# High parts of the first twelve exponential blocks on GpSimd, and the constant row's additions in the feature stage

## The chip, the cores and the metric

The kernel runs on one core of a Trainium2 chip. The core's engines work side by side, each through its own queue in order, and wait for one another by semaphores: TensorE (PE in the profile; PEld is its weight load), VectorE (DVE), ScalarE (ACT), GpSimd (POOL) and SyncE (SP), which issues most of the DMAs. The metric is the device time of one execution in microseconds (us), lower being better.

## What is computed

A transformer block with two parts, each behind a layer norm and a residual addition: an attention whose scores are distances between three-dimensional positions, causal, with sixteen heads that share them, and a mixture of eight experts with top 2 beside a shared expert. The change touches the attention alone. Cut to it:

```python
x = x + attn(layernorm(x))               # x: (2, 2048, 256)
x = x + ffn(layernorm(x))                # gate, 8 experts, top 2, 2 shared

def attn(x):
    V = x @ wv.T + bv
    pos = x @ w3d.T + b3d                # (2, 2048, 3)
    dist = pairwise_l2(pos)
    scores = -dist * 0.25                # the same for all heads
    scores = where(causal, -inf, scores)
    out = softmax(scores) @ V
    return out @ wo.T + bo
```

All is float32, and the attention's output projection is folded into the value matrix, as the scores are the same for all heads.

## The kernel before

**Tiling.** A batch has S = 2048 tokens, in TB = 16 tiles of 128, four tiles (GT) to a group, GB = 4 groups. The residual stream of both batches stays in `X` in SBUF. The attention runs for batch 0 and then for batch 1 (`for b in range(NB)` on each engine). Products of float32 precision are made of three matmuls on values that are split into a high part, rounded to the type that TensorE reads (fp32r), and a low part, the difference.

**The feature stage.** TensorE transposes and multiplies for values and positions, VectorE and ScalarE split them into `VO`. VectorE then writes 45 small instructions (`N_POS`, each counting up `s_f`) into `FQ`, `FKh` and `FKl`, from which TensorE makes `QT`, `KTh`, `KTl`. In batch 0 VectorE ends this stage with `shift` (L518), the constant row (bias terms) that has to be added to every tile of X.

**The distance stage.** `sq_blocks` lists 40 blocks of squared distances, key tile kt by query group Q, in two halves: Q = 0 and 1, then Q = 2 and 3. TensorE makes one with two matmuls (L658, L659), VectorE evicts it from PSUM into `E` (L523). GpSimd masks the 16 diagonal blocks with two `affine_select` each (`diagonal`, L267 to L274). ScalarE takes the roots of a half row by row (L349) and then the exponentials of that half block by block, in place (L356, `s_exp`).

**The value stage.** `blocks` lists the same 40 blocks in the order of the groups: Q = 0 has 4, Q = 1 has 8, Q = 2 has 12, Q = 3 has 16. They are 512 queries wide, the last four of a group 512, 384, 256 and 128. For each one a high part goes into the ring `E_hi` (NE = 8 buffers) and a low part into `E_lo`, and TensorE multiplies with `VO` (L674, L676, L678: three matmuls for each 128 queries, so 12 for a full block). Who writes the high part depends on the block:

- blocks 0 to 11 (`N_HI_DVE` = 12, the groups of the first half): VectorE, by `split_hi` (L540 to L544), one block ahead of the low part. It counts `s_eh`.
- blocks 12 to 39: ScalarE, by `high_part` (L336 to L340), three blocks behind its exponentials. It counts `s_eh_act`.

The low part of every block is VectorE's (`split_lo`, L546 to L553). Behind a block's low part VectorE may have a `finish` (L525 to L538): when a group's sums are complete, a tile is divided by its denominator, added to X and has its statistics taken. That is done for group Q - 1 within the first three blocks of group Q (two in the third), and needs the tile's constant row added (`s_xc`). A buffer of the ring is free when TensorE has ended the block eight before (`s_eb`, which starts at 8). TensorE's first value matmul stands behind all 40 distance blocks.

In batch 0 VectorE also takes the statistics of batch 1 between the low parts, from block 18 on.

**GpSimd's order in a batch** (L257 to L283): memsets of `FQ`, `FKh`, `FKl` (in batch 1 once batch 0's value stage is over), diagonals 0 to 7, then the constant row's additions for tiles 0 to 11 (`add_shift`, L262 to L265), diagonals 8 to 15, and the additions for tiles 12 to 15. It issues no DMA in the attention.

Of the kernel before, what the change touches and what calls it, by code (L numbers as in the profile page):

```python
# [7 lines left out]
TB = S // P  # L8
GT = 4
# [7 lines left out]
N_FQ, N_FKH, N_POS = 30, 34, 45  # L17
# [34 lines left out]
def attention_and_experts(nc, x, wv, bv, woT, bo, w3dT, b3d, gateT, gate_bias, wT, sw13T, sw2T, out):  # L52
# [19 lines left out]
    with ExitStack() as ctx:  # L72
# [127 lines left out]
        def block_of(Q, kt):  # L200
# [9 lines left out]
        halves = [range(0, GB // 2), range(GB // 2, GB)]  # L210
        sq_blocks = [(Q, kt) for half in halves for kt in range(GT * half[-1] + GT)
                     for Q in range(max(kt // GT, half[0]), half[-1] + 1)]
        N_HI_DVE = blocks.index((halves[1][0], 0))
        AHEAD = 3
        N_STAT = NBLK - 6 - TB
        NROW = sum(GT * half[-1] + GT for half in halves)
# [24 lines left out]
        @block.gpsimd  # L241
        def _(pool):
            pool.memset(ident[:, :], 0.0).then_inc(s_const, 1)
            pool.memset(one_f[:, :], 1.0).then_inc(s_const, 1)
            pool.memset(eps_col[:, :], EPS).then_inc(s_const, 1)
            pool.memset(mean_of[:, :], 1.0 / D).then_inc(s_const, 1)
            pool.memset(w3_raw[:, :, 3:MW - D], 0.0).then_inc(s_const, 1)
            pool.memset(one_zero[:, :, 0], 1.0).then_inc(s_const, 1)
            pool.memset(one_zero[:, :, 1], 0.0).then_inc(s_const, 1)
            pool.memset(blank[:, :], 0.0).then_inc(s_const, 1)  # L250
            pool.iota(no_row[:, :], pattern=[[P, NSLOT]], base=TOPK * NT * P, channel_multiplier=1,
                      allow_small_or_imprecise_dtypes=True).then_inc(s_const, 1)
            pool.wait_ge(s_const, 9)
            pool.memset(blank[:, FIRST:FIRST + 1], -1.0).then_inc(s_const, 1)
            pool.affine_select(out=ident[:, :], in_=ident[:, :], compare_op=ALU.not_equal, fill=1.0, base=0,
                               pattern=[[-1, P]], channel_multiplier=1).then_inc(s_const, 1)
            for b in range(NB):  # L257
                if b > 0:
                    pool.wait_ge(s_eb, b * NBLK + NE)
                for F in (FQ, FKh, FKl):  # L260
                    pool.memset(F[:, :, :], 0.0).then_inc(s_fz, 1)
                def add_shift(tiles):  # L262
                    for t in tiles:
                        pool.tensor_tensor(tile_of(X, b * TB + t), tile_of(X, b * TB + t), shift[:, :], ALU.add)\
                            .then_inc(s_xc, 1)  # L265

                def diagonal(kt):  # L267
                    blk = E[:, off(kt):off(kt) + P]
                    pool.wait_ge(s_e2, b * NBLK + sq_blocks.index((kt // GT, kt)) + 1 + NQ)
                    pool.affine_select(out=blk, in_=blk, compare_op=ALU.is_ge, fill=1.0e30, base=0,  # L270
                                       pattern=[[1, P]], channel_multiplier=-1).then_inc(s_diag, 1)
                    pool.wait_ge(s_diag, 2 * (b * TB + kt) + 1)
                    pool.affine_select(out=blk, in_=blk, compare_op=ALU.not_equal, fill=0.0, base=0,
                                       pattern=[[1, P]], channel_multiplier=-1).then_inc(s_diag, 1)  # L274

                half = GT * len(halves[0])
                for kt in range(half):
                    diagonal(kt)
                pool.wait_ge(s_shift, 1)
                add_shift(range(TB - GT))  # L280
                for kt in range(half, TB):
                    diagonal(kt)
                add_shift(range(TB - GT, TB))  # L283

        @block.scalar
        def _(act):
# [8 lines left out]
            for b in range(NB):  # L295
                def deviation(g0, n):
                    tiles = slice(g0 * GT, (g0 + n) * GT)
                    act.wait_ge(s_mv, TB * b + (g0 + n) * GT)
                    act.activation(std[:, tiles], mv[:, tiles, 1], ACT.Sqrt, bias=eps_col[:, 0:1]).then_inc(s_std, n)

                def group_hi(g):
                    for c in range(KC):
                        act.wait_ge(s_T, KC * (b * GB + g) + c + 1)
                        act.activation(XT_hi[:, g % 2, c, :], T_ps[g % 2][c][:, :], ACT.Copy).then_inc(s_xth, 1)

                group_hi(0)
                if b == 0:
                    deviation(0, 1)
                    for c in range(KC):
                        act.wait_ge(s_Mps, c + 1)  # L310
                        act.activation(M_hi[:, c, 0:D], M_ps[c][:, 0:D], ACT.Copy).then_inc(s_chi, 1)
                else:
                    deviation(0, GB)
                for g in range(GB):
                    if g + 1 < GB:
                        group_hi(g + 1)
                        if b == 0:
                            deviation(g + 1, 1)
                    act.wait_ge(s_rstd, b * GB + g + 1)
                    for j in range(GT):  # L320
                        t = g * GT + j
                        act.wait_ge(s_vps[j % 2], 2 * (b * GB + g) + j // 2 + 1)
                        act.activation(VO[:, t, 0:D], V_ps[j][:, 0:D], ACT.Copy, scale=rstd[:, t:t + 1])\
                           .then_inc(s_voh, 1)
                if b == 0:
                    act.wait_ge(s_bcol, 16)
                    for c in range(KC):
                        act.activation(bv_all[:, c, :], bv_col[:, c:c + 1].to_broadcast([P, P]), ACT.Copy)\
                           .then_inc(s_bv, 1)
                for k, dst in enumerate((QT, KTh, KTl)):  # L330
                    for g in range(GB):
                        n = GB * k + g
                        act.wait_ge(s_ft, 3 * GB * b + n + 1)
                        act.activation(dst[:, g * 512:(g + 1) * 512], Q_ps[n % 4][:, :], ACT.Copy)\
                           .then_inc(s_fr, 1)
                def high_part(n):  # L336
                    blk, _, w = block_of(*blocks[n])
                    act.wait_ge(s_exp, b * NBLK + n + 1)
                    act.wait_ge(s_eb, b * NBLK + n + 1)
                    act.activation(E_hi[:, n % NE, 0:w], blk, ACT.Copy).then_inc(s_eh_act, 1)  # L340

                rows = n = 0
                for half in halves:
                    for kt in range(GT * half[-1] + GT):
                        row = row_of(half, kt)

                        act.wait_ge(s_e2, b * NBLK + sq_blocks.index((half[-1], kt)) + 1 + NQ)
                        act.wait_ge(s_diag, 2 * (b * TB + kt) + 2)
                        act.activation(row, row, ACT.Sqrt).then_inc(s_dist, 1)  # L349
                    rows += GT * half[-1] + GT  # L350

                    act.wait_ge(s_dist, b * NROW + rows)
                    for Q in half:
                        for kt in range(GT * Q + GT):
                            blk = block_of(Q, kt)[0]
                            act.activation(blk, blk, ACT.Exp, scale=-SCALE).then_inc(s_exp, 1)  # L356
                            if n - AHEAD >= N_HI_DVE:
                                high_part(n - AHEAD)
                            n += 1
                for n in range(NBLK - AHEAD, NBLK):  # L360
                    high_part(n)

        @block.vector
        def _(dve):
# [63 lines left out]
            for b in range(NB):  # L428
# [108 lines left out]
                    dve.wait_ge(s_x1, t + 1 + 2 * GT)  # L537
                    dve.bn_stats(st1[:, t, :], tile_of(X, t))  # L538

                def split_hi(n):  # L540
                    blk, _, w = block_of(*blocks[n])
                    dve.wait_ge(s_exp, b * NBLK + n + 1)
                    dve.wait_ge(s_eb, b * NBLK + n + 1)
                    dve.tensor_copy(E_hi[:, n % NE, 0:w], blk).then_inc(s_eh, 1)  # L544

                def split_lo(n):  # L546
                    blk, _, w = block_of(*blocks[n])
                    if n < N_HI_DVE:
                        dve.wait_ge(s_eh, b * N_HI_DVE + n + 1)
                    else:  # L550
                        dve.wait_ge(s_eh_act, (b + 1) * (NBLK - N_HI_DVE) + n + 1 - NBLK)
                    dve.tensor_tensor(E_lo[:, n % NE, 0:w], blk, E_hi[:, n % NE, 0:w].bitcast(f32),  # L552
                                      ALU.subtract).then_inc(s_el, 1)  # L553

                split_hi(0)
                for n, (Q, kt) in enumerate(blocks):
                    if n + 1 < N_HI_DVE:
                        split_hi(n + 1)
                    split_lo(n)
                    if b + 1 < NB and 0 <= n - N_STAT <= TB:  # L560
                        statistics(b + 1, n - N_STAT)
# [945 lines left out]
```

## Time and profile before

| | us |
|---|---|
| time before, median of 3 runs | 629.19 (628.64 to 632.95) |
| the profiled execution's own time | 628.38 |
| its span, first to last instruction | 626.6 |
| granted TensorE clock, mean | 0.961 |

The page of the profile gives, for that execution, the busy time of each engine, the span in 40 slices, the queues, the chain of work that ended last and the costliest groups of instructions. From the trace come timelines (instructions in order of time, equal neighbours merged, with the count behind an x), stretches (busy time of each engine in a given piece of the span) and groups of instructions. Times are us from the span's start. A line number such as L552 is that of the kernel before. An idle time in brackets is the engine's own ahead of the instruction, with what ended it. The attention of batch 0 takes about the first 122 us, that of batch 1 the next 110; the distance stages lie at 46 to 67 and 154 to 175, the value stages behind them.

### The profile page before, as it was taken

Reading aid. Unit: us, or ns where it says so; the run is one execution under the profiler, and the core shown is the slowest. Engines: PE = TensorE matmul, PEld = TensorE weight load, DVE = VectorE, ACT = ScalarE, POOL = GpSimd, SP = SyncE. Lnnn points to the kernel's source line nnn. Section 1 sums busy time; section 2 is a strip of 40 time slices with the busy share of each in tenths; the row PEclk is TensorE's granted clock in tenths of the full one; section 3 lists DMA queues with packets and bytes.
Section 4 is the critical chain, followed back from the end, with each engine's and each line's share of the span. In section 5 each row is a group of like instructions: output and inputs, shape, how many; then the busy total and the mean of one; then the engine's idle time right before and its main releaser. Section 6 shows DMA issues by size and latency. Waiting matters only on the chain.

```text
span 626.6 us, 11501 instructions
## 1 busy us (share of the span) xinstructions
PE 553.8 (88%) x3468; PEld 480.2 (77%) x3468; DVE 452.1 (72%) x1226; ACT 330.2 (53%) x684; POOL 283.5 (45%) x569
## 2 busy tenths in 40 slices
PE   5869799996989979838999998999999999998885
PEld 4856699986579975527888887888888888887764
DVE  7949999584999737586776654666666666664795
ACT  3548978264997805514445432455555555554321
POOL 4007500120840015006676661477667777665690
PEclk9979899997989997977999999899999999999999
DMA  8999000000000009302222222233333333331994
GB/s 266 329 315 14 1 1 2 1 1 2 0 2 1 2 3 378 124 1 86 87 87 87 95 87 61 69 107 109 103 103 107 108 104 109 105 105 60 321 329 155
DMA packets 57130, 63.03 MB, mean 101 GB/s; under 512 B 14737, under 2 KB 50449, under 8 KB 57073
## 3 DMA queue, kind: packets, MB, share of 16 engines
q1 hardware_dynamic: 49216, 43.75, 24.6%
q0 software_dynamic: 6480, 17.90, 8.1%
q10 hardware_dynamic: 1376, 0.66, 0.4%
q8 instruction: 31, 0.51, 0.4%
q14 instruction: 27, 0.21, 0.1%
HBM read 30.64 MB, written 31.65 MB: 99 GB/s over the span
## 4 chain that ended last, share of the span: by engine, by line
PE 54%; DVE 6%; issue 1%; ACT 1%; POOL 0%; DVEq 0%; POOLq 0%
PE bank L1312 16%; PE bank L1314 15%; PE bank L1313 15%; PE bank L1435 3%; PE bank L1451 2%; PE bank L1320 1%; PE bank L1364 1%; DVE h_lo L1242 1%; DVE XN L1086 1%; DVE X L1225 0%; PE bank L1337 0%; DVE X L1215 0%; DVE mv L1083 0%; DVE hf L1234 0%; DVE XT_lo L1124 0%
## 5 line engine op out<-in xcount | busy, mean ns | idle before, releaser
L968 POOL DMA_INDIRECT token_out<-YS,to_row x71 | 71.7, 1010 | 49.4 <-DVE back L1279 46.0
L932 POOL DMA_INDIRECT slots_in<-X,slot x64 | 66.1, 1033 | 60.6 <-DVE slot L1199 30.6
L674 PE MATMUL a_bank<-VO,E_hi 128*128 128x258 f32 x272 | 79.2, 291 | 8.7 <-DVE E_lo L552 6.1
L678 PE MATMUL a_bank<-VO,E_lo 128*128 128x258 f32 x272 | 78.2, 288 | 0.0
L676 PE MATMUL a_bank<-VO,E_hi 128*128 128x256 f32 x272 | 78.0, 287 | 0.0
L1268 DVE TENSOR_TENSOR hr<-bank,sr 128x256 f32<-128x256 f32 x71 | 30.1, 425 | 60.1 <-ACT sr L1045 60.1
L1312 PE MATMUL bank<-W_hi,XST_hi 128*128 x142 | 62.4, 440 | 0.5 <-DVE XST_lo L1284 0.5
L1045 ACT ACTIVATE sr<-bank 128x256 f32<-128x256 f32 x71 | 27.2, 383 | 63.9 <-PE bank L1314 63.9
L674 PEld LDWEIGHTS a_bank<-VO,E_hi 128*128 128x128 f32 x272 | 52.9, 194 | 10.2 <-DVE E_lo L552 7.5
L1019 ACT ACTIVATE h_hi<-hf 128x512 fp32r<-128x512 f32 x32 | 20.2, 632 | 73.2 <-DVE hf L1234 73.2
L1313 PE MATMUL bank<-W_lo,XST_hi 128*128 x142 | 56.8, 400 | 0.0
L1314 PE MATMUL bank<-W_hi,XST_lo 128*128 x142 | 56.3, 397 | 0.0
L1312 PE MATMUL bank<-XT_hi,sw_hi 128*128 128x512 f32 x128 | 51.6, 403 | 3.3 <-DVE XT_lo L1124 1.7
L523 DVE TENSOR_SCALAR E<-a_bank 128x512 f32<-128x512 f32 (+3 forms) x80 | 41.6, 597 | 16.0 <-PE a_bank L659 16.0
L678 PEld LDWEIGHTS a_bank<-VO,E_lo 128*128 128x128 f32 x272 | 52.9, 194 | 0.0
L676 PEld LDWEIGHTS a_bank<-VO,E_hi 128*128 128x128 f32 x272 | 52.8, 194 | 0.0
L1312 PE MATMUL bank<-sw_hi,h_hi 128*128 128x256 f32 x128 | 37.4, 293 | 17.1 <-DVE h_lo L1242 16.0
L1313 PE MATMUL bank<-XT_lo,sw_hi 128*128 128x512 f32 x128 | 50.6, 395 | 0.0
L552 DVE TENSOR_TENSOR E_lo<-E,E_hi 128x512 fp32r<-128x512 f32 (+1 forms) x80 | 48.2, 631 | 3.1 <-ACT E_hi L340 3.1
L1314 PE MATMUL bank<-XT_hi,sw_lo 128*128 128x512 f32 x128 | 50.4, 394 | 0.0
L1312 PE MATMUL bank<-W_hi,hT_hi 128*128 x142 | 45.9, 323 | 0.0
L1057 ACT ACTIVATE YS<-bank,by_weight 128x256 f32<-128x256 f32 x71 | 33.6, 474 | 20.0 <-PE bank L1314 20.0
(247 smaller groups left out, 1680.9 us busy)
## 6 DMA issues: line engine op xcount, KB each, us to landing
XS<-slots_in SPq DMA_DIRECT2D x71, 131.0 KB, 2.1
slots_in<-blank SPq DMA_DIRECT2D x7, 1179.0 KB, 14.0
YG<-token_out SPq DMA_DIRECT2D x16, 512.0 KB, 8.8
W_raw<-in_wT_dram SPq DMA_DIRECT2D x8, 768.0 KB, 13.9
X<-in_x_dram SPq DMA_DIRECT2D x8, 512.0 KB, 8.3
out_dram<-X SPq DMA_DIRECT2D x32, 128.0 KB, 1.9
token_out<-YS,to_row POOLq DMA_INDIRECT x71, 2.5
slots_in<-blank SPq DMA_DIRECT2D x1, 1048.0 KB, 14.3
```

What stands on the lines that cost most here:

```text
L523: dve.tensor_scalar(blk, Q_ps[n % NQ][:, 0:w], 0.0, None, ALU.max).then_inc(s_e2, 1)
L552: dve.tensor_tensor(E_lo[:, n % NE, 0:w], blk, E_hi[:, n % NE, 0:w].bitcast(f32), ALU.subtract).then_inc(s_el, 1)
L674: pe.matmul(O_ps[Q % 2][j][:, 0:D + 2], E_hi[:, n % NE, cols], VO[:, kt, 0:D + 2], start=(kt == 0), stop=False)
L676: pe.matmul(O_ps[Q % 2][j][:, 0:D], E_hi[:, n % NE, cols], VO[:, kt, D + 2:VW], start=False, stop=False)
L678: mm = pe.matmul(O_ps[Q % 2][j][:, 0:D + 2], E_lo[:, n % NE, cols], VO[:, kt, 0:D + 2], start=False, stop=(kt == qt))
L932: pool.indirect_dma_start(out=xs, out_offset=bass.IndirectOffsetOnAxis(ap=slot[k][:, t:t + 1], axis=0), in_=X[:, t, :], in_offset=None).th ...
L968: pool.indirect_dma_start(out=ys, out_offset=bass.IndirectOffsetOnAxis(ap=to_row[:, i:i + 1], axis=0), in_=YS[:, i % NYS, :], in_offset=No ...
L1057: act.activation(YS[:, i % NYS, :], Y_ps[v][:, 0:D], ACT.Copy, scale=by_weight[:, i:i + 1])\
L1268: dve.tensor_tensor(hr[:, v, :], S_ps[v][:, D:2 * D], sr[:, v, :], ALU.mult).then_inc(s_hr, 1)
L1312: pe.matmul(out, a_hi, b_hi, start=start, stop=False, **kw)
L1313: pe.matmul(out, a_hi, b_lo, start=False, stop=False, **kw)
L1314: return pe.matmul(out, a_lo, b_hi, start=False, stop=stop, **kw)
```

## The change

GpSimd gets a function `high_part` that copies a block of E into `E_hi`, with the waits that `split_hi` had. It writes the high parts of blocks 0 to 11 of each batch, and `split_hi` is gone from VectorE, where only the low parts stay. GpSimd's order in a batch becomes: memsets; then a wait for all 45 feature instructions of the batch and for `shift`; additions for tiles 0 to 11; diagonals 0 to 7; additions for tiles 12 to 15; high parts 0 to 7; diagonals 8 to 15; high parts 8 to 11. The constant is renamed to `N_HI_POOL`, its value 12 stays.

```diff
--- before.py
+++ after.py
@@ -210,7 +210,7 @@
         halves = [range(0, GB // 2), range(GB // 2, GB)]
         sq_blocks = [(Q, kt) for half in halves for kt in range(GT * half[-1] + GT)
                      for Q in range(max(kt // GT, half[0]), half[-1] + 1)]
-        N_HI_DVE = blocks.index((halves[1][0], 0))
+        N_HI_POOL = blocks.index((halves[1][0], 0))
         AHEAD = 3
         N_STAT = NBLK - 6 - TB
         NROW = sum(GT * half[-1] + GT for half in halves)
@@ -273,14 +273,25 @@
                     pool.affine_select(out=blk, in_=blk, compare_op=ALU.not_equal, fill=0.0, base=0,
                                        pattern=[[1, P]], channel_multiplier=-1).then_inc(s_diag, 1)
 
+                def high_part(n):
+                    blk, _, w = block_of(*blocks[n])
+                    pool.wait_ge(s_exp, b * NBLK + n + 1)
+                    pool.wait_ge(s_eb, b * NBLK + n + 1)
+                    pool.tensor_copy(E_hi[:, n % NE, 0:w], blk).then_inc(s_eh, 1)
+
                 half = GT * len(halves[0])
+                pool.wait_ge(s_f, N_POS * (b + 1))
+                pool.wait_ge(s_shift, 1)
+                add_shift(range(TB - GT))
                 for kt in range(half):
                     diagonal(kt)
-                pool.wait_ge(s_shift, 1)
-                add_shift(range(TB - GT))
+                add_shift(range(TB - GT, TB))
+                for n in range(NE):
+                    high_part(n)
                 for kt in range(half, TB):
                     diagonal(kt)
-                add_shift(range(TB - GT, TB))
+                for n in range(NE, N_HI_POOL):
+                    high_part(n)
 
         @block.scalar
         def _(act):
@@ -354,7 +365,7 @@
                         for kt in range(GT * Q + GT):
                             blk = block_of(Q, kt)[0]
                             act.activation(blk, blk, ACT.Exp, scale=-SCALE).then_inc(s_exp, 1)
-                            if n - AHEAD >= N_HI_DVE:
+                            if n - AHEAD >= N_HI_POOL:
                                 high_part(n - AHEAD)
                             n += 1
                 for n in range(NBLK - AHEAD, NBLK):
@@ -537,25 +548,16 @@
                     dve.wait_ge(s_x1, t + 1 + 2 * GT)
                     dve.bn_stats(st1[:, t, :], tile_of(X, t))
 
-                def split_hi(n):
-                    blk, _, w = block_of(*blocks[n])
-                    dve.wait_ge(s_exp, b * NBLK + n + 1)
-                    dve.wait_ge(s_eb, b * NBLK + n + 1)
-                    dve.tensor_copy(E_hi[:, n % NE, 0:w], blk).then_inc(s_eh, 1)
-
                 def split_lo(n):
                     blk, _, w = block_of(*blocks[n])
-                    if n < N_HI_DVE:
-                        dve.wait_ge(s_eh, b * N_HI_DVE + n + 1)
+                    if n < N_HI_POOL:
+                        dve.wait_ge(s_eh, b * N_HI_POOL + n + 1)
                     else:
-                        dve.wait_ge(s_eh_act, (b + 1) * (NBLK - N_HI_DVE) + n + 1 - NBLK)
+                        dve.wait_ge(s_eh_act, (b + 1) * (NBLK - N_HI_POOL) + n + 1 - NBLK)
                     dve.tensor_tensor(E_lo[:, n % NE, 0:w], blk, E_hi[:, n % NE, 0:w].bitcast(f32),
                                       ALU.subtract).then_inc(s_el, 1)
 
-                split_hi(0)
                 for n, (Q, kt) in enumerate(blocks):
-                    if n + 1 < N_HI_DVE:
-                        split_hi(n + 1)
                     split_lo(n)
                     if b + 1 < NB and 0 <= n - N_STAT <= TB:
                         statistics(b + 1, n - N_STAT)
```

## Rows read from the trace of the kernel before

**Rows 1.** The page, part 1: busy us (share of span), instructions by engine.

```profile
PE 553.8 (88%) x3468; PEld 480.2 (77%) x3468; DVE 452.1 (72%) x1226; ACT 330.2 (53%) x684; POOL 283.5 (45%) x569
```

**Rows 2.** Stretch of batch 0, behind block 7's start: busy by engine, clock.

```profile
84.00:119.00 35.00, 35.00 (x295) 35.00 (x294) 28.99 (x84) 22.44 (x45) 0.00 (x0) 1.00 0.00 1
```

**Rows 3.** PE's timeline, batch 0: start, duration, line, operation, tiles, count, [idle].

```profile
66.62 0.28 PE L659 MATMUL a_bank<-QT,KTl 128*128 128x128 f32 x1
...
69.49 0.55 PE L674 MATMUL a_bank<-VO,E_hi 128*128 128x258 f32 x1 [2.58 <-issue]
...
70.27 0.42 PE L674 MATMUL a_bank<-VO,E_hi 128*128 128x258 f32 x1
...
71.55 0.42 PE L674 MATMUL a_bank<-VO,E_hi 128*128 128x258 f32 x1
...
81.35 0.39 PE L674 MATMUL a_bank<-VO,E_hi 128*128 128x258 f32 x1 [1.33 <-DVE E_lo L552]
```

**Rows 4.** The same view, batch 1.

```profile
174.87 0.27 PE L659 MATMUL a_bank<-QT,KTl 128*128 128x128 f32 x1
...
177.68 0.39 PE L674 MATMUL a_bank<-VO,E_hi 128*128 128x258 f32 x1 [2.54 <-DVE E_lo L552]
...
189.61 0.39 PE L674 MATMUL a_bank<-VO,E_hi 128*128 128x258 f32 x1 [1.33 <-DVE E_lo L552]
```

**Rows 5.** VectorE's timeline, batch 0, from the evictions to block 18.

```profile
47.19 20.80 DVE L523 TENSOR_SCALAR E<-a_bank 128x512 f32<-128x512 f32 x40 [7.48 <-PE a_bank L659]
67.92 0.77 DVE L544 CAST E_hi<-E 128x512 fp32r<-128x512 f32 x2
68.61 0.77 DVE L552 TENSOR_TENSOR E_lo<-E,E_hi 128x512 fp32r<-128x512 f32 x1
...
72.08 0.82 DVE L552 TENSOR_TENSOR E_lo<-E,E_hi 128x128 fp32r<-128x128 f32 x1
...
78.18 0.16 DVE L532 RECIPROCAL rden<-a_bank 128x1 f32<-128x1 f32 x1
...
79.23 0.15 DVE L532 RECIPROCAL rden<-a_bank 128x1 f32<-128x1 f32 x1
...
89.44 2.48 DVE L552 TENSOR_TENSOR E_lo<-E,E_hi 128x512 fp32r<-128x512 f32 x4
```

**Rows 6.** Short stretches of PE: length, busy, granted clock, DMA, GB/s.

```profile
68.00:69.00 1.00, 0.00 (x0) 0.94 0.03 8
...
72.00:73.00 1.00, 1.00 (x9) 0.85 0.00 0
...
178.00:178.50 0.50, 0.50 (x5) 0.61 0.00 0
```

**Rows 7.** The same view, batch 1: the distance evictions.

```profile
155.43 20.80 DVE L523 TENSOR_SCALAR E<-a_bank 128x512 f32<-128x512 f32 x40 [8.53 <-PE a_bank L659]
```

**Rows 8.** GpSimd's casts of the next stage: count | busy, mean ns | idle.

```profile
L926 POOL CAST sw_hi<-sw_raw 128x2048 fp32r<-128x2048 f32 x1 | 1.9, 1893 | 7.0 <-DMA sw_raw<-in_sw2T_dram 7.0
L926 POOL CAST sw_hi<-sw_raw 128x1024 fp32r<-128x1024 f32 x1 | 1.0, 1039 | 0.0
```

**Rows 9.** Timeline of GpSimd, batch 0.

```profile
48.03 0.29 POOL L270 TENSOR_SCALAR_AFFINE_SELECT E<-E 128x128 f32<-128x128 f32 x1 [40.39 <-DVE E L523]
...
54.45 7.81 POOL L264 TENSOR_TENSOR X<-X,shift 128x256 f32<-128x256 f32 x12
...
63.17 0.29 POOL L270 TENSOR_SCALAR_AFFINE_SELECT E<-E 128x128 f32<-128x128 f32 x1 [0.92 <-DVE E L523]
...
70.36 3.04 POOL L264 TENSOR_TENSOR X<-X,shift 128x256 f32<-128x256 f32 x4
```

**Rows 10.** Timeline of ScalarE, batch 0.

```profile
56.20 5.08 ACT L356 ACTIVATE E<-E 128x512 f32<-128x512 f32 x12
...
62.59 12.28 ACT L349 ACTIVATE E<-E 128x1024 f32<-128x1024 f32 x16
...
78.28 0.62 ACT L340 ACTIVATE E_hi<-E 128x512 fp32r<-128x512 f32 x1
```

## The prediction

> **What bounds the kernel now.** I read the page first: over the whole span PE is busy 88% and VectorE 72% [rows 1], so the change can pay only where PE waits for VectorE. The stretches and timelines of the attention stage say where that is. From block 7 of a batch on, PE is busy without a gap: 35.00 of 35 us with 295 matmuls [rows 2], which gives a pitch of 35.00 / 295 = 0.1186 us at the full clock, or 1.42 us for a block of twelve. Ahead of that it waits. In batch 0 the last distance matmul ends at 66.62 + 0.28 = 66.90, the first value matmul starts only at 69.49, and block 7 starts at 81.35 after a wait of 1.33 for `E_lo` [rows 3]. Blocks 0 to 6 hold 12 + 9 + 6 + 3 + 36 = 66 matmuls, 66 x 0.1186 = 7.83 us of work, yet 81.35 - 69.49 = 11.86 us pass. Batch 1 repeats it: 175.14, 177.68, 189.61 [rows 4].
>
> VectorE is what PE waits for. It evicts the last distance block at about 67.9, then casts two high parts (0.77 for both), writes `E_lo` of block 0 by 69.38, and goes on without idling: cast, `E_lo`, and a `finish` per block [rows 5]. Each 512-wide `E_lo` costs it 0.60 pitch ((2.48 - 0.68) / 3) and each `finish` 79.23 - 78.18 = 1.05 [rows 5]. The seven casts of blocks 1 to 7 and the one of block 0 are the work the change takes off this chain.
>
> One more thing sits there. TensorE's granted clock falls from 2.4 to 1.2 GHz during the wait: at about 68.88 (the 0.94 of the stretch 68 to 69) and back at about 72.30, 3.42 us at half, and in batch 1 from 178.11 [rows 6]. At half clock six matmuls take 71.55 - 70.27 = 1.28, a pitch of 0.213 [rows 3]. Now this is hidden, because VectorE is the slower of the two; afterwards it isn't.
>
> **The change, part by part.**
>
> *1. Twelve casts a batch leave VectorE (L544).* `E_lo` of block 0 becomes the first instruction behind the evictions, at 67.92 [rows 5]. I give it the 0.77 that it takes now with GpSimd's diagonals beside it, and PE starts 0.11 behind its end, as now (69.38 to 69.49): 67.92 + 0.77 + 0.11 = 68.80, so 0.69 earlier. In batch 1 the evictions start at 155.43 and take the same 20.80 [rows 7], so the next instruction is issued 67.92 - 47.19 = 20.73 later, at 176.16, and PE starts at 176.16 + 0.88 = 177.04, or 0.64 earlier.
>
> When could block 7 start? By PE alone at 68.80 + 7.83 = 76.63. By VectorE: `E_lo` of blocks 0 to 4 at 0.60 each (the narrow ones are cheaper, which leaves room for the diagonals), four `finish` (4.20), `E_lo` 5 to 7 (1.80): 67.92 + 3.00 + 4.20 + 1.80 + 0.11 = 77.03. By PE with the clock at half for 3.42 us: 3.42 x (1 - 0.1186 / 0.213) = 1.52 us are lost, 76.63 + 1.52 = 78.15. So batch 0 gains 81.35 - 78.15 = 3.20 if the clock falls in it, 4.32 if it doesn't; batch 1 gains 189.61 - (177.04 + 7.83 + 1.52 = 186.39) = 3.22, or about 4.3.
>
> Will the clock fall? PE's pause shrinks from 2.59 to 1.90 (66.90 to 68.80). In batch 0 it fell 1.98 after the last matmul ended, in batch 1 2.97 after [rows 3, 4, 6]; the pause of 1.33 before block 7 is followed by a clock of 1.00 [rows 2, 3]. The new pause lies between. I take one batch of the two with a fall.
>
> *2. The casts on GpSimd.* The nearest rows are its f32 to fp32r casts of the next stage: 1.89 us for 2048 columns, 1.04 for 1024 [rows 8]. On that line 512 columns cost 0.19 + 512 x 0.00083 = 0.61. Upper bound: its additions of 256 columns, 7.81 / 12 = 0.65 each [rows 9], twice that for 512 with a second operand, 1.30.
>
> Blocks 0 to 7: their exponentials run from 56.20 to 61.28 for twelve, about 59.8 for the eighth [rows 10]. GpSimd is free of its last four additions at 54.45 + 4 x 0.65 = 57.05, and eight casts take at most 8 x 0.61 = 4.9, to 62.0. Diagonal 8 can't start before 63.17 anyway, because its distance block isn't evicted [rows 9]. Cost nothing; the cover is 1.2 us, and behind it another: ScalarE's root of row 8 starts at about 62.59 + 8 x 0.88 = 69.6 (the first rows are the widest, estimated from the merged row's 12.28 for 16) [rows 10]. At 1.30 a cast the diagonals would be 4.3 late and still in time for it.
>
> Blocks 8 to 11 wait for PE to release a buffer, that is for the ends of blocks 0 to 3 (71.3 to 74 with the slow clock), and GpSimd is through its diagonals at 70.36, where its last additions begin now [rows 9]. They end by about 74.6; VectorE wants the first at 77. Hidden. Nothing else is queued behind them until the next batch's memsets, which wait for PE's last block as now.
>
> *3. Contention.* VectorE's `E_lo` of 128 columns took 0.82 at 72.08 [rows 5] with GpSimd's last additions (70.36 to 73.40) beside it [rows 9], against 0.60 for four times the columns when GpSimd is quiet. The casts of blocks 8 to 11 can so hold `E_lo` 5 and 6, at most 0.61 each, and move 77.03 to at most 78.25; the last four additions, which did this until now, are gone from there. A batch whose clock stays up then gains between 3.1 and 4.3, and I take the middle, 3.8 for a warm batch.
>
> The Trainium skill, SBUF — State Buffer, section "SBUF: two separate sides", says that a GpSimd instruction and a VectorE one with two SBUF inputs take a shared port pair in turns, the loser standing still for the whole instruction. The trace agrees (that 0.82). By the rule in full the warm batches gain 3.1 and not 3.8.
>
> *4. The additions of the constant row.* Twelve move ahead of the diagonals. They wait for VectorE's last feature instruction and, in batch 0, for `shift` behind it. VectorE has done both when its idle time ahead of the evictions begins, at 47.19 - 7.48 = 39.71 [rows 5]. The additions take 7.81: to 47.5, with diagonal 0 starting at 48.03 after 40.39 idle [rows 9]. In batch 1 they can start at 155.43 - 8.53 = 146.90 [rows 7] and end at 154.7, before the first eviction. Cost nothing; the cover is 0.5 us in batch 0, and a miss by that much moves only ScalarE, which is 3 us ahead at block 12 (below). No DMA is issued by any moved instruction, and the queues of SP and ACT are not touched.
>
> *5. What comes next.* After block 7 the suppliers must keep 3 to 4 us more ahead. ScalarE's high part of block 12 starts at 78.28 and takes 0.62 [rows 10], its time set by roots and exponentials that don't move; PE wants block 12 at 77.1 + 42 x 0.1186 = 82.1 at the earliest. VectorE from there: `E_lo` 12 at 78.9, then four `finish` and `E_lo` 12 to 15, 4.2 + 2.4 = 6.6, to 85.5; PE wants block 15 at 82.1 + 36 x 0.1186 = 86.4. It holds by 0.9. After that VectorE has 0.60 plus 0.6 of statistics per 1.42. So the gain stays to the end of the batch, and both batches feed one chain.
>
> **Sum.** 3.2 (fallen clock) + 3.8 (clock kept) = 7.0 us off the profiled execution's 628.38 (span 626.6 and 1.8 around it): 621.4. The median shown is 0.81 above that execution, so I forecast 629.19 - 7.0 = 622.2. That is 1.1%; about 1% is what a measurement of this kernel can tell from no change.
>
> **The rivals.**
> *Both clocks fall, or neither.* 3.2 + 3.2 = 6.4 gives 622.8, just over the bound; neither, at the best 4.3 + 4.3 = 8.6, gives 620.6. Same mechanism, other size.
>
> *VectorE is late a second time* (blocks 12 to 15, or `E_lo` 5 to 7 held longer than one cast each). For it: the margin of 0.9. Against: ScalarE's parts are ready 3 us early. If 1 to 2 us a batch are given back: gain 3 to 5, 624.2 to 626.2.
>
> *GpSimd's casts hold the distance evictions.* Eight casts run beside L523, which alone sets the pace of the distance stage. If each held an eviction for its 0.61, a batch would lose 4.9 against 3.2 won: 2 x 1.7 = 3.4 slower, 632.6. It decides from 3.2 / 8 = 0.40 per cast. Against it: twelve additions, which read and write SBUF too, run beside those evictions now, 7.8 us of them, and the clean pitch stays at 0.52 (20.80 for 40) [rows 5, 9].
>
> The Trainium skill, GPSIMD Engine Reference, section "Engine selection", would keep elementwise work on VectorE, with two-input operations about twice as slow on GpSimd and one-input ones near line rate. The trace's 0.00083 us per column for the cast agrees with the second half.
>
> **How the numbers follow.** Forecast with its three clock cases 0.66; given back in part 0.24; slower 0.05; better than all of it 0.05. The low end is 620.6 less 0.6 for the spread of medians, 620.0; the high end reaches the worst of the second rival, 626.2. Faster by over 1% (below 622.9) takes most of the first case, not all, since both-fall lies on the bound: 0.54. Within 1%: 0.42. Slower: 0.04.
>
> **What would show it.** `CAST E_hi` appears on POOL 24 times at about 0.61 for 512 columns and is gone from VectorE; eight of them end before 63.2; L523 still takes 20.8 for 40. First value matmul near 68.8 after a pause of 1.9, block 7 near 77 to 78.2 without a wait ahead of it. It is wrong if the last evictions come later than 67.9, if PE still waits for `E_lo` at blocks 5 to 7, or if a new wait for `E_lo` stands at blocks 12 to 16.

## The result, and the profile after

| | before | after |
|---|---|---|
| median, us | 629.86 (628.64 to 632.95) | 622.37 (621.86 to 623.46) |
| profiled execution, us | 628.38 | 621.86 |
| its span, us | 626.6 | 620.1 |

The ratio is 0.9897 with a 95% interval of 0.9873 to 0.9920, so the changed kernel is 1.0% faster, by 6.5 us. The two medians lie 7.5 apart; the times before scatter by over 4 us, so the ratio is what counts. The median before is now over four executions, one more than in the table of the time before. Six further executions of the changed kernel (e1) gave 0.9901.

The page's first part. VectorE has 24 instructions fewer and GpSimd 24 more; against [rows 1] 11.0 us of busy time left VectorE, more than the casts alone would take undisturbed (0.22 to 0.41 us each, by width, where nothing ran beside them in the trace before; about 8.3 us for all 24):

```profile
PE 552.9 (89%) x3468; PEld 480.1 (77%) x3468; DVE 441.1 (71%) x1202; ACT 329.1 (53%) x684; POOL 291.3 (47%) x593
```

PE's timeline of the changed kernel at the head of the value stage of batch 0, then of batch 1. It answers to [rows 3, 4]. L661 is the distance matmul, L676 the value matmul. The third row of the first view is block 7's first matmul. The pause is 1.80 and 1.75 us where it was 2.58 and 2.54, and behind it there is no wait for `E_lo` any more:

```profile
66.12 0.28 PE L661 MATMUL a_bank<-QT,KTl 128*128 128x128 f32 x1
68.19 0.36 PE L676 MATMUL a_bank<-VO,E_hi 128*128 128x258 f32 x1 [1.80 <-issue]
...
77.68 0.28 PE L676 MATMUL a_bank<-VO,E_hi 128*128 128x258 f32 x1
```

```profile
171.07 0.27 PE L661 MATMUL a_bank<-QT,KTl 128*128 128x128 f32 x1
173.09 0.39 PE L676 MATMUL a_bank<-VO,E_hi 128*128 128x258 f32 x1 [1.75 <-DVE E_lo L557]
```

VectorE's timeline, batch 0, answering to [rows 5]: the same 20.80 us for the 40 evictions, and the low parts of blocks 0 to 4 directly behind them.

```profile
46.69 20.80 DVE L534 TENSOR_SCALAR E<-a_bank 128x512 f32<-128x512 f32 x40 [7.50 <-PE a_bank L661]
67.42 2.66 DVE L557 TENSOR_TENSOR E_lo<-E,E_hi 128x512 fp32r<-128x512 f32 x5
```

GpSimd's timeline, batch 0, answering to [rows 9]. The additions end before diagonal 0, eight casts take 3.87 us, and diagonal 8 still waits, 2.31 us, for its eviction:

```profile
39.34 7.75 POOL L264 TENSOR_TENSOR X<-X,shift 128x256 f32<-128x256 f32 x12 [31.68 <-DVE shift L529]
47.53 0.29 POOL L270 TENSOR_SCALAR_AFFINE_SELECT E<-E 128x128 f32<-128x128 f32 x1 [0.44 <-DVE E L534]
...
56.49 3.87 POOL L280 CAST E_hi<-E 128x512 fp32r<-128x512 f32 x8
62.67 0.29 POOL L270 TENSOR_SCALAR_AFFINE_SELECT E<-E 128x128 f32<-128x128 f32 x1 [2.31 <-DVE E L534]
...
71.05 1.15 POOL L280 CAST E_hi<-E 128x512 fp32r<-128x512 f32 x1 [0.82 <-PE a_bank L680]
```

And the granted clock in short stretches of PE (length, busy and count, clock, DMA share, GB/s), answering to [rows 6]. It falls in both batches, and in both when PE is already back at work: at about 68.42 in batch 0 (0.2 us after the first value matmul) and at about 174.2 in batch 1 (1.1 us after it):

```profile
68.00:69.00 1.00, 0.81 (x5) 0.71 0.00 0
71.00:72.00 1.00, 1.00 (x7) 0.59 0.00 0
173.00:174.00 1.00, 0.91 (x7) 1.00 0.03 8
174.00:175.00 1.00, 1.00 (x8) 0.61 0.00 0
```

**Where the 6.5 us are.** Whole-kernel times scatter by a microsecond or two, and a part of that lies ahead of the first distance stage (its evictions start at 46.69 here, at 47.19 before, and at 47.85 in the same kernel's second profile). A yardstick without that is the length of a value stage, from VectorE's first instruction behind the evictions to PE's first waiting instruction of the next stage. For before that is 124.71 - 67.92 = 56.79 us in batch 0 and 234.77 - 176.16 = 58.61 in batch 1; after, 120.95 - 67.42 = 53.53 and 227.66 - 172.36 = 55.30. The four ends in PE's timelines, before and then after:

```profile
124.71 0.39 PE L598 MATMUL a_bank<-M_hi,XT_hi 128*128 128x260 f32 x1 [1.21 <-DVE XT_lo L397]
...
234.77 1.09 PE L1320 MATMUL bank<-ident,X 128*128 128x128 f32 x8 [3.87 <-POOL before L921]
```

```profile
120.95 0.39 PE L600 MATMUL a_bank<-M_hi,XT_hi 128*128 128x260 f32 x1 [1.21 <-DVE XT_lo L408]
...
227.66 1.09 PE L1322 MATMUL bank<-ident,X 128*128 128x128 f32 x8 [3.87 <-POOL before L923]
```

So the value stages give 3.26 + 3.31 = 6.57 us. Of the rest of the span, the earlier start gives 0.50, and the expert part and the end are about 0.6 longer in this execution, which no edit touches. In the further profiles below, kernels with the same value stage repeat its length within 0.03 us.

### The profile page after: what moved, and what is told of

Read it like the earlier page. It is cut to its first block, busy times and chain, and to the rows that moved or that the text cites. A ratio compares the mean times of both kernels' runs of the same rounds, so it can differ in the third digit from the quotient of the medians.

```text
span 620.1 us, 11503 instructions
## 1 busy us (share of the span) xinstructions
PE 552.9 (89%) x3468; PEld 480.1 (77%) x3468; DVE 441.1 (71%) x1202; ACT 329.1 (53%) x684; POOL 291.3 (47%) x593
## 4 chain that ended last, share of the span: by engine, by line
PE 55%; DVE 6%; issue 1%; ACT 1%; POOL 0%; DVEq 0%; POOLq 0%
PE bank L1314 16%; PE bank L1316 15%; PE bank L1315 15%; PE bank L1437 3%; PE bank L1453 2%; PE bank L1322 1%; PE bank L1366 1%; DVE h_lo L1244 1%; DVE XN L1088 1%; DVE X L1227 0%; PE bank L1339 0%; DVE mv L1085 0%; DVE X L1217 0%; DVE hf L1236 0%; DVE XT_lo L1126 0%
## 5 line engine op out<-in xcount | busy, mean ns | idle before, releaser
L676 PE MATMUL a_bank<-VO,E_hi 128*128 128x258 f32 x272 | 78.5, 289 | 3.5 <-issue 1.8
L676 PEld LDWEIGHTS a_bank<-VO,E_hi 128*128 128x128 f32 x272 | 53.0, 195 | 3.8 <-issue 1.9
L557 DVE TENSOR_TENSOR E_lo<-E,E_hi 128x512 fp32r<-128x512 f32 (+1 forms) x80 | 45.6, 609 | 4.9 <-ACT E_hi L351 4.9
```

The source lines that it names most:

```text
L676: pe.matmul(O_ps[Q % 2][j][:, 0:D + 2], E_hi[:, n % NE, cols], VO[:, kt, 0:D + 2], start=(kt == 0), stop=False)
```

## The experiments

All lengths of the value stages at a glance. "Clock falls" counts the batches in which the granted clock goes to 1.2 GHz at the head of the value stage.

| kernel | batch 0 | batch 1 | clock falls | median, us | ratio to before |
|---|---|---|---|---|---|
| before | 56.79 | 58.61 | 2 | 629.86 | 1 |
| after | 53.53 | 55.30 | 2 | 622.37 | 0.9897 (0.9873 to 0.9920) |
| after again (e1) | 53.55 | 55.33 | 2 | 622.80 | 0.9901 (0.9884 to 0.9918) |
| additions alone (e3) | 54.81 | 56.58 | 2 | 625.18 | 0.9935 (0.9912 to 0.9959) |
| casts alone (e4) | 53.61 | 55.37 | 2 | 623.87 | 0.9910 (0.9891 to 0.9929) |
| casts twice (e6) | 53.57 | 55.37 | 2 | 622.55 | 0.9893 (0.9876 to 0.9909) |
| before, pause filled (e5) | 56.82 | 58.62 | 0 | 630.19 | 1.0015 (1.0004 to 1.0027) |
| additions alone, filled (e8) | 54.81 | 56.57 | 0 | 626.92 | 0.9900 (0.9863 to 0.9938) |
| after, filled with 7 (e2) | 52.09 | 53.89 | 0 | 619.70 | 0.9841 (0.9820 to 0.9863) |
| the same again | 52.10 | 53.89 | 0 | 618.94 | 0.9840 (0.9823 to 0.9857) |
| after, filled with 3 (e9) | 52.11 | 53.87 | 0 | 624.14 | 0.9864 (0.9827 to 0.9900) |
| more pauses filled (e7) | 52.08 | 53.88 | 0 | 616.61 | 0.9792 (0.9773 to 0.9811) |

Each ratio is to the kernel before as it ran beside that run, not to the 629.86 in the table. While e8 and e9 ran the chip was slower and less steady: the kernel before took 632.64 (629.74 to 636.29), and 628.97 and 629.39 beside the others. For these two the ratios and the value stages are to be read, not the medians.

**The changed kernel again (e1).** No edit.

> The changed kernel once more, as the measure for the runs beside it. Theory A (VectorE's casts were PE's limit at the head of each value stage, and what is left there is the half clock): 622 to 623 us, ratio to the kernel before 0.989 to 0.990, PE without a wait for E_lo between block 1 and block 39. In its trace the pause of PE ahead of block 0 is 1.75 to 1.8 us in both batches and the clock falls in or just behind it in most of them.

622.80, ratio 0.9901. The value stages agree with the first profile within 0.03 us, and the clock fell in both batches again.

**The additions alone (e3).** VectorE keeps its casts; GpSimd's order is the new one without the high parts.

```diff
-                for kt in range(half):
-                    diagonal(kt)
+                pool.wait_ge(s_f, N_POS * (b + 1))
                 pool.wait_ge(s_shift, 1)
                 add_shift(range(TB - GT))
-                for kt in range(half, TB):
+                for kt in range(half):
                     diagonal(kt)
                 add_shift(range(TB - GT, TB))
+                for kt in range(half, TB):
+                    diagonal(kt)
```

> The kernel before with only the additions of the constant row moved as in the change; VectorE keeps its casts. Theory A (the casts' time on VectorE is what counts): E_lo and casts at the head of the value stage lose their overlap with GpSimd's last four additions, about 1.4 us of the 0.77 to 0.86 us instructions come back to 0.41 and 0.68; 1.0 to 1.5 us a batch, 2 to 3 us in all, 626.5 to 627.5. Rival D (the gain of the change came from taking GpSimd's additions out of VectorE's way and not from moving the casts): 623 to 624, near the whole gain. Rival E: nothing, 629.

1.98 and 2.03 us less in the value stages, 3.8 in the median: more than theory A's 2 to 3, less than rival D's near-whole gain. VectorE's casts show how. Its timeline in e3 has the casts of blocks 4 and 5, alone on their ports, at 0.41; before, the one that began at 71.30 took 0.86:

```profile
71.92 0.41 DVE L545 CAST E_hi<-E 128x512 fp32r<-128x512 f32 x1
```

```profile
71.30 0.86 DVE L544 CAST E_hi<-E 128x512 fp32r<-128x512 f32 x1
```

PE's waits for low parts in e3 are three, 2.9 us together. 2.5 of these are the pause ahead of block 0 in batch 1; the other two stand ahead of block 7, 0.20 and 0.21 us where there were 1.33. So VectorE still sets the start of block 7, but PE with its fallen clock is almost as late:

```profile
PE a_bank L675 <- DVE E_lo L553: 2.9, 3, 2.5
```

```profile
80.53 0.39 PE L675 MATMUL a_bank<-VO,E_hi 128*128 128x258 f32 x1 [0.20 <-DVE E_lo L553]
```

**The casts alone (e4).** The high parts on GpSimd, the additions where they were.

```diff
-                pool.wait_ge(s_f, N_POS * (b + 1))
-                pool.wait_ge(s_shift, 1)
-                add_shift(range(TB - GT))
                 for kt in range(half):
                     diagonal(kt)
-                add_shift(range(TB - GT, TB))
+                pool.wait_ge(s_shift, 1)
+                add_shift(range(TB - GT))
                 for n in range(NE):
                     high_part(n)
                 for kt in range(half, TB):
                     diagonal(kt)
+                add_shift(range(TB - GT, TB))
```

> The changed kernel with the additions of the constant row where they were before (twelve behind diagonal 7, four behind diagonal 15). GpSimd then runs 7.8 us later: its first high part at about 62.3 and not 57, diagonal 8 at 66.4 and not 63.2, the last additions at 72 to 75, the high part of block 8 at about 75. Theory A (there is cover: ScalarE's root of row 8 comes at 69.6, VectorE's first low part at 67.9, its low part of block 8 at 77): within 1 us of the changed kernel, 622.5 to 623.5, E_lo of blocks 0 to 7 up to 0.3 us longer each while the additions run. Rival D (the move of the additions matters by itself): 1 us a batch or more is lost, above 624.5.

The value stages are 0.08 and 0.07 us longer than with the whole change, which is theory A. The median, 623.87, is 0.4 above theory A's range and 1.1 above e1 beside it; the value stages don't hold that difference, and in the two profiles 1.06 us of it lies ahead of the first eviction (48.91 against 47.85), where no run looked for its cause. The two halves of the change don't add up: additions alone give 2.0 a batch, casts alone 3.2, both together 3.3. Once the casts are gone, VectorE has room to be held up by the additions: in the changed kernel its low part of block 7 starts at 75.67 and takes 0.68, and PE starts on it only at 77.68, 1.3 us later. GpSimd ran as late as expected (its timeline, batch 0: casts at 63.90, the last additions at 74.14, and the four high parts behind them at 77.16), and nobody paid for it: ScalarE waited 2.6 us for its diagonals in batch 0, 3.1 in the changed kernel, and no low part came late for PE:

```profile
56.16 7.79 POOL L264 TENSOR_TENSOR X<-X,shift 128x256 f32<-128x256 f32 x12
63.90 3.87 POOL L280 CAST E_hi<-E 128x512 fp32r<-128x512 f32 x8
...
74.14 3.08 POOL L264 TENSOR_TENSOR X<-X,shift 128x256 f32<-128x256 f32 x4
77.16 2.56 POOL L280 CAST E_hi<-E 128x512 fp32r<-128x512 f32 x4
```

**The casts twice (e6).** The changed kernel with

```diff
+                    pool.tensor_copy(E_hi[:, n % NE, 0:w], blk).then_inc(s_once, 1)
+                    pool.wait_ge(s_once, b * N_HI_POOL + n + 1)
                     pool.tensor_copy(E_hi[:, n % NE, 0:w], blk).then_inc(s_eh, 1)
```

> The changed kernel with each of GpSimd's twelve casts a batch made twice. The first eight then end about 4.4 us later, near 64.8 in the changed kernel's time, and diagonal 8 starts 2 us later than its distance block allows. Theory A (the casts are covered by ScalarE's roots and by the ring): the same as the changed kernel within 0.5 us, 622.3 to 623.3, the 40 evictions still at 20.8. Rival G (a cast on GpSimd holds an eviction or a low part of VectorE): 0.4 to 0.6 us for each of the additional casts beside it, 3 us a batch, 625 or more.

622.55, value stages within 0.07 us of the changed kernel's. Rival G is out: sixteen casts beside the evictions leave them at 20.81 for 40. A 512-wide cast takes 0.61, a 128-wide one 0.29:

```profile
58.87 0.61 POOL L283 CAST E_hi<-E 128x512 fp32r<-128x512 f32 x1
...
61.60 0.29 POOL L283 CAST E_hi<-E 128x128 fp32r<-128x128 f32 x1
```

```profile
48.36 20.81 DVE L537 TENSOR_SCALAR E<-a_bank 128x512 f32<-128x512 f32 x40 [7.57 <-PE a_bank L664]
```

**The pause filled (e2, and again).** Behind the distance loop of TensorE:

```diff
+                for _ in range(7):
+                    pe.matmul(bank[7][:, :], KTh[:, 0:P], QT[:, 0:512], start=True, stop=True)
                 if b == 0:
                     pe.wait_ge(s_shift, 1)
```

> The changed kernel with seven more matmuls of 512 columns behind the last distance block of each batch, into a PSUM bank that nobody reads then; they are work the reference doesn't ask for and fill 7 x 0.23 = 1.6 us of PE's pause of 1.8. Theory A (the half clock is now what the head of the value stage pays, 3.42 us at a pitch of 0.213 and not 0.119, that is 1.5 us a batch): the clock stays at full, block 7 starts 1.1 to 1.5 us earlier in each batch, 2.2 to 3.0 us less in all, 619.3 to 620.2. Rival B (VectorE is at once the limit again, because block 7's E_lo is ready only just before PE wants it): the clock stays at full but PE waits at blocks 5 to 7, and less than 0.8 us is won. Rival C (the clock isn't governed by PE's own pause): it falls all the same, and nothing is won.

> The changed kernel with seven matmuls in the pause ahead of the value stage once more, beside the one that fills more pauses. 619.3 to 620.3; ratio to the kernel before 0.983 to 0.986.

1.44 and 1.41 us less in the value stages than the changed kernel, 3.1 in the median, 0.9841 and 0.9840 of the kernel before (the second median, 618.94, is 0.4 below its range). Rivals B and C are out: the clock is 1.00 at the head of both value stages, and PE is at work for all but 0.1 of ten microseconds. PE's timeline with the filling and the stretches behind it, in the second of the two runs:

```profile
66.56 1.84 PE L664 MATMUL a_bank<-QT,KTh 128*128 128x512 f32 x7
```

```profile
67.00:77.00 10.00, 9.88 (x77) 1.00 0.01 2
169.00:179.00 10.00, 9.93 (x75) 1.00 0.01 2
```

But rival B's condition is nearly met. In the first of the two runs VectorE's low part of block 7, the first of the five in this row, ends at 77.79 + 0.68 = 78.47, and PE starts on the block at 78.54, 0.07 us later (the same in batch 1). So with the clock kept the two engines arrive together, and a PE faster still would win next to nothing here:

```profile
77.79 2.28 DVE L557 TENSOR_TENSOR E_lo<-E,E_hi 128x512 fp32r<-128x512 f32 x5
```

```profile
78.54 0.36 PE L678 MATMUL a_bank<-VO,E_hi 128*128 128x258 f32 x1
```

**The same in the kernel before (e5)**, with ten matmuls for its longer pause.

> The kernel before with ten matmuls of 512 columns behind the last distance block of each batch (work the reference doesn't ask for, into a bank nobody reads then), 10 x 0.23 = 2.3 us of PE's pause of 2.6. Theory A (there VectorE is the slower one at the head of the value stage, so the half clock of TensorE is hidden): the clock stays at full and the time is that of the kernel before within 0.5 us, with longer waits of PE for E_lo between block 1 and block 7. Rival F (the half clock was already paid before the change): 2 to 3 us less.

Value stages +0.03 and +0.01, ratio 1.0015 (median 0.8 above the kernel before beside it, where 0.5 was allowed; the value stages don't show it). The clock stays at full, and PE only waits more. Before and then in e5, its waits for low parts; 2.54 of the 6.1 are the pause ahead of block 0 in batch 1, so 3.5 became 5.5:

```profile
PE a_bank L674 <- DVE E_lo L552: 6.1, 6, 2.5
```

```profile
PE a_bank L676 <- DVE E_lo L552: 5.5, 9, 1.3
```

So the half clock cost nothing before the change and costs 1.4 us a batch after it.

**The additions alone, pause filled (e8)**, the edits of e3 and e5 together.

> The kernel before with the additions moved (VectorE keeps its casts) and ten matmuls more in PE's pause of 2.6 us. It tells what the casts themselves are worth once the clock is kept. Theory A: with the casts on VectorE its chain sets block 7 (its low part at 79.8 + 0.68 in the run with the additions moved alone, PE's own time there with a full clock 1.5 us earlier), so the kept clock brings less than 0.5 us a batch: 624.3 to 625.3, and the casts on GpSimd are then worth 2.5 us a batch, the difference to the changed kernel with its pause filled (618.9 to 619.7). Rival H (PE's pace with the half clock is the limit in that kernel too): 1.5 us a batch less, 622 to 622.5, and the casts are worth 1.3 a batch as without the filling.

The value stages are those of e3 to 0.01 us. With the casts on VectorE its chain is the limit, clock or no clock; rival H is out. PE waits 1.3 us for block 7's low part again:

```profile
PE a_bank L677 <- DVE E_lo L553: 3.0, 4, 1.3
```

Against e2 the casts are worth 54.81 - 52.09 = 2.72 and 2.68 us a batch when the clock is kept, and 1.28 (54.81 - 53.53) when it falls. The ratio, 0.9900, came out better than e3's 0.9935 and by itself would fit rival H; their intervals overlap, the value stages rule H out, and a part of the difference lies between the two value stages (50.87 us against 51.54 in e3), where in the feature stage of batch 1 the clock falls 1.8 us and returns 1.4 us earlier.

**Three matmuls and not seven (e9).** `range(3)`.

> The changed kernel with three matmuls and not seven in the pause, 0.7 us of 1.8, so that PE still rests 1.1 us ahead of the value stage. If a rest of 1.1 us is short enough for the clock (PE's rests of 1.0 to 1.3 us ahead of the distance stage are followed by a full clock) the clock stays at full and the time is that with seven, 619 to 620. If it falls in one batch or both, 620.5 to 622.5.

Value stages as with seven, ratio 0.9864 (0.9827 to 0.9900; the seven had 0.984). After a rest of 1.05 us in batch 0 and 1.00 in batch 1 the clock stays at full:

```profile
69.62 0.36 PE L678 MATMUL a_bank<-VO,E_hi 128*128 128x258 f32 x1 [1.05 <-issue]
```

**More pauses filled (e7).** On top of e2, 8 matmuls of 260 columns ahead of the first transpose of the position maximum, and 18 (batch 0) or 28 (batch 1) behind its spreading:

```diff
+                for _ in range(8):
+                    pe.matmul(bank[7][:, 0:MW], XT_hi[:, 1, 0, 0:P], M_hi[:, 0, :], start=True, stop=True)
                 pe.wait_ge(s_f, N_POS * b + 1)
...
+                for _ in range(28 if b > 0 else 18):
+                    pe.matmul(bank[7][:, 0:MW], XT_hi[:, 1, 0, 0:P], M_hi[:, 0, :], start=True, stop=True)
                 for k, (F, ready) in enumerate(((FQ, N_FQ), (FKh, N_FKH), (FKl, N_POS))):
```

> The kernel with the filled pause (seven matmuls behind the distance blocks), and 26 more of 260 columns in batch 0 and 36 in batch 1 in PE's two pauses in the feature stage, where the clock falls too and the twelve copies of QT, KTh and KTl by ScalarE wait for transposes at half clock. Theory A (the clock follows PE's own activity): full clock there, the first QT copies at 0.6 and not 0.86 pitch, about 1 us a batch less than with the seven alone. Rival: the fillers run at half clock, last longer than the pauses and delay the transposes by up to 2 us a batch.

616.61, 0.9792 (0.9773 to 0.9811), 2.3 us less than e2 beside it, where about 1 was expected. The clock is 1.00 through both feature stages. ScalarE's timeline shows the copies of `QT` back to back (four in 2.07 us); in the changed kernel the first three started 0.86 and 0.85 apart. The value stages stay those of e2. From PE's transpose of the position maximum to the first eviction it took 13.89 and 13.79 us in e2 and 12.59 in both batches here, so the gain lies in the feature stages. It is the fastest version tried, 2.1% below the kernel before.

```profile
39.11 2.07 ACT L345 ACTIVATE QT<-a_bank 128x512 fp32r<-128x512 f32 x4 [6.21 <-PE a_bank L656]
```

```profile
38.86 0.60 ACT L345 ACTIVATE QT<-a_bank 128x512 fp32r<-128x512 f32 x1 [6.67 <-PE a_bank L652]
39.72 0.60 ACT L345 ACTIVATE QT<-a_bank 128x512 fp32r<-128x512 f32 x1 [0.26 <-PE a_bank L652]
```

## Why the prediction was right, and where it wasn't

The forecast was 7.0 us, 622.2; measured are 6.5 us by the ratio and 622.37. The mechanism was right. That the sum came so close is in part luck, as the clock's term was wrong and two sizes were off.

**What binds the head of the value stage.** Right. VectorE did (e5 and e8: a kept clock brings nothing while the casts are there), and PE with its half clock does afterwards (e2: a kept clock brings 1.4 us a batch).

**The start of block 0.** Forecast 0.88 behind the end of the evictions; it came 68.19 - 67.42 = 0.77 and 173.09 - 172.36 = 0.73 behind. The 0.77 for the first low part, borrowed from a row with a neighbour on the port, was too much; it took 0.68.

**Gain with a fallen clock, 3.20 and 3.22.** Measured 3.26 and 3.31 over the value stage. Block 7 was forecast 10.23 us behind the end of the evictions and came 77.68 - 67.42 = 10.26 behind, in batch 1 too; block 0 came 0.1 earlier than forecast and the seven blocks took 0.14 to 0.18 longer. This term carried the result.

**"I take one batch of the two with a fall."** Wrong: the clock fell in both batches in all four profiles with a pause of about 1.8 us and nothing in it (after, e1, e4, e6). I had counted the 1.98 us between the last matmul and the fall as a distance that a pause of 1.90 might stay under. The falls don't move with the pause: before, they came 1.98 and 2.97 us after the last distance matmul ended, now at 68.42 - 66.40 = 2.0 and 174.2 - 171.3 = 2.9, with 0.8 us less pause. In batch 1 PE had resumed before the fall already in the rows before (177.68 against 178.11), so the length of the pause alone could not have told me.

**The warm batch, 3.8.** Mis-sized: with the clock kept a batch gains 56.79 - 52.09 = 4.70 and 58.61 - 53.89 = 4.72. Two terms were too pessimistic. VectorE's five low parts were put at 3.00 and took 2.58 (five in e2 from 69.80 to the `finish` at 72.38), as the narrow ones are cheaper, which makes 0.4. The allowance for low parts 5 and 6 held by GpSimd's casts took off another 0.5, and neither was held in e2 (0.67 and 0.68 in batch 0). No batch of the changed kernel was warm, so this term stood in the sum for a second cold one. One cold and one warm batch of the right size would have made 3.2 + 4.7 = 7.9, 1.4 too much; the warm term being 0.9 too small brought the sum back to 7.0. That is luck. Both cold had been forecast at 6.4, and 6.5 came.

**GpSimd's casts hidden, at 0.61.** Right (0.61 in e6, eight in 3.87 in the change). Even twice as many are hidden.

**Contention.** Right in kind, too large in size. In e1 the low part of block 5 took 1.12 us with GpSimd's cast of block 8, 0.61, beside it; 0.68 is its time alone. In the first profile it was the cast that gave way, 1.15 us. Neither reached PE. The rule of the Trainium skill, SBUF — State Buffer, section "SBUF: two separate sides", that one of the two waits out the other's instruction, fits each of these.

```profile
72.20 1.12 DVE L557 TENSOR_TENSOR E_lo<-E,E_hi 128x512 fp32r<-128x512 f32 x1
```

```profile
72.17 0.61 POOL L280 CAST E_hi<-E 128x512 fp32r<-128x512 f32 x1 [0.79 <-PE a_bank L680]
```

**The additions at no cost.** Right, with 0.44 us of cover in batch 0 where 0.5 was forecast. What the prediction left out is that their move is worth 2.0 us a batch by itself while VectorE does the casts (e3), and 0.07 beside the rest of the change (e4). I had seen the additions stretch VectorE's instructions and never priced that.

**What comes next.** Right: no wait of PE for a low part behind block 0, at blocks 12 to 16 neither in the changed kernel nor with the clock kept (e2). At block 7 the margin is 1.3 us in the changed kernel and 0.07 in e2.

**Open.** What the clock answers to isn't settled by these runs; they show only that the pause of 1.8 us was followed by a fall in eight of eight batches and the one of 1.0 (e9) in neither of two, and two batches are few. Whether the fillers cost anything elsewhere isn't settled either: e5 was 0.8 us slower in the median, outside its value stages. How the 2.3 us of e7 divide between the two places that it fills wasn't tried.

## What to carry to other kernels

When you relieve the engine that TensorE waits for at the start of a stage, ask what TensorE will pay once it is the limit itself: here a half clock that had been free cost 1.4 us a batch as soon as VectorE was relieved, and three spare matmuls in the pause took it back. Two edits that relieve the same chain don't add, so try each alone: here the simpler one, moving GpSimd's additions out of VectorE's way, brought 60% of the gain in the value stages. And measure a stage between two marks within it: the value stage repeated to 0.1 us where the kernel's time scattered by 1 to 2.

## What the runs showed of the hardware

- The granted clock can fall after the pause is over: in the changed kernel PE had been back at work for 0.2 us in batch 0 and for 1.1 us in batch 1. It stayed at half for 3.4 us in both (68.4 to 71.8 and 174.2 to 177.6) although PE was busy. The stretch of the changed kernel in which it returns:

```profile
177.00:178.00 1.00, 1.00 (x8) 0.68 0.00 0
```

- Casts and additions of GpSimd leave VectorE's evictions from PSUM alone (20.80 to 20.81 for 40 in all runs, with 12 additions, 8 casts or 16 casts beside them), while a VectorE cast between SBUF tiles went from 0.41 to 0.86 beside GpSimd's additions and a low part from 0.68 to 1.12 beside one of its casts.
- GpSimd's f32 to fp32r cast took 0.29 us at 128 columns and 0.61 at 512 without a neighbour on the port; the line through 1024 and 2048 columns in [rows 8] had given 0.61.
